# The last stage of a graph layer: part of v added on VectorE instead of GpSimd, and results added one step earlier

## The chip, the cores and the metric

The kernel runs on one core of a Trainium2 chip. The metric is the device time of one execution in microseconds. A core has five engines with instruction queues of their own: TensorE (PE, matmuls), VectorE (DVE), ScalarE (ACT), GpSimd (POOL) and SyncE (SP, which here only issues DMAs). Each queue runs in order, and queues meet at semaphores. TensorE's clock has two levels, 1.2 and 2.4 GHz; the profile shows the granted share of the upper one.

## The reference

One layer of a graph network over B = 16 graphs, N = 1024 nodes, D = 256 features, all in float32:

```
pre_u  = h @ W1[:d];  pre_v = h @ W1[d:]
hidden = relu(pre_u[:, :, None, :] + pre_v[:, None, :, :] + b1)       # b u v k
S      = sigmoid(hidden @ W2 + b2)                                    # b u v
a_t    = einsum('buv,bud->bvd', S * A, h)
m_t    = einsum('uv,bud->bvd', A, h) * h
out    = beta1 * h + beta2 * (a_t @ Wa + ba) + beta3 * (m_t @ Wm + bm)
```

A is 1024 x 1024 and mostly zero. h is the input x.

## The kernel before

Everything but the last sum over u is done ahead: `hWa_dram` holds beta2 * h @ Wa, `base_dram` all terms of the output that don't depend on S, and `sum_dram` (u, v, b) the part of the gate's argument that is not linear. The linear parts are kept apart: `of_u`, in on-chip memory for good, and `of_v`, a tile of 128 v by 16 b that is the same in all 128 partitions and is loaded anew for each group.

The last stage, the only one that the change touches, works on 64 tiles of 128 u by 128 v, each for 16 graphs. Eight tiles with the same v make a group (`vt`), `t` counts the u tiles in it, and `k = 8 * vt + t`. A tile passes four engines:

- SyncE loads `raw[k % 2]` (1 MB of `sum_dram`, L1440) and `adj_b[k % 5]` (64 KB of A, L1442). In group 0 it also loads `hWa_all` for that t (2 MB, L1444), which stays for all groups. At t == 0 it first waits until all adds of the group before are done and loads `of_v` (1 MB, L987). At t == 4 it waits until the results of the group before are stored, and loads `z` (2 MB of `base_dram`, L1447).
- GpSimd adds `of_v` to `raw` and writes the sum, turned from (v, b) to (b, v), into one of four buffers `masked[k % 4]` (L1457). It waits until TensorE is done with tile k - 4 (`step_done`).
- ScalarE applies the sigmoid, 16 instructions (L1513). After t == 3 it issues the store of `z` of the group before (L1505).
- VectorE multiplies by `adj_b` (L1475). After t == 1 it calls `finish(vt - 1)`: eight additions of 512 elements that add PSUM to `z` (L1466).
- TensorE: 16 products of 128 x 128 by 128 x 256, each as two matmul instructions, into eight PSUM banks that add up over the eight tiles of a group (L1493). At t == 0 each pair of products waits until `finish` has taken the old contents of its bank.

No order is written out but that of each queue's program. Semaphores: `raw_added` counts the adds, `gate_made` the sigmoids, `gate_masked` the masks, `gate_used` and `z_summed` TensorE's tiles, `z_ready` the z additions.

Of the kernel before, what the change touches and what calls it, by code (L numbers as in the profile page):

```python
# [5 lines left out]
def gnn_edges_kernel(nc, x, adj, W1, b1, W2, b2, Wa, ba, Wm, bm, beta1, beta2, beta3, out):  # L6
# [15 lines left out]
    ALU = mybir.AluOpType  # L22
# [43 lines left out]
    with ctx:  # L66
# [919 lines left out]
        def load_of_v(sp, vt):  # L986
            sp.dma_start(of_v[:].rearrange("p v b -> p (v b)"), linear_dram[1, vt * P:(vt + 1) * P, :]  # L987
                         .rearrange("(a v) b -> a (v b)", a=1).broadcast_to([P, P * B])).then_inc(of_v_loaded, 16)
# [408 lines left out]

        work.close()
        with ExitStack() as phase:
            RAW, GM, ADJ = 2, 4, 5  # L1400
            hWa_all = sb("hWa_all", [P, NT, B, D], scope=phase)
            raw = [sb(f"raw{i}", [P, P, B], scope=phase) for i in range(RAW)]
            adj_b = [sb(f"adj_b{i}", [P, P], scope=phase) for i in range(ADJ)]
            masked = [sb(f"masked{i}", [P, B, P], scope=phase) for i in range(GM)]
            z = sb("z", [P, B, D], scope=phase)
            z_psum = [pb(f"z_psum{i}", [P, BANK], scope=phase) for i in range(B // 2)]
            raw_loaded = [sem(f"raw_loaded{i}") for i in range(RAW)]
            adj_loaded = [sem(f"adj_loaded{i}") for i in range(ADJ)]
            hWa_loaded = [sem(f"hWa_loaded{i}") for i in range(NT)]
            u_ready = sem("u_ready")  # L1410
            raw_added = sem("raw_added")
            gate_made = sem("gate_made")
            z_loaded = sem("z_loaded")
            gate_masked = sem("gate_masked")
            gate_used = sem("gate_used")
            z_summed = sem("z_summed")
            z_ready = sem("z_ready")
            z_stored = sem("z_stored")
            sum_uv = sum_dram.rearrange("(u v) b -> u v b", v=N)

            def step_done(eng, k):
                vt, t = divmod(k, NT)
                if k < 0:
                    return
                if t == NT - 1:
                    eng.wait_ge(z_summed, (B // 2) * (vt + 1))
                else:
                    eng.wait_ge(gate_used, (NT - 1) * vt + t + 1)  # L1428

            with nc.Block() as block:  # L1430
                @block.sync
                def _(sp):
                    for vt in range(NT):
                        for t in range(NT):
                            k = vt * NT + t
                            if t == 0 and vt:
                                sp.wait_ge(raw_added, k)
                                load_of_v(sp, vt)
                            waits(sp, raw_added, k - RAW + 1)
                            sp.dma_start(raw[k % RAW][:], sum_uv[t * P:(t + 1) * P, vt * P:(vt + 1) * P, :]).then_inc(raw_loaded[k % RAW], 16)  # L1440
                            waits(sp, gate_masked, k - ADJ + 1)
                            sp.dma_start(adj_b[k % ADJ][:], adj[t * P:(t + 1) * P, vt * P:(vt + 1) * P]).then_inc(adj_loaded[k % ADJ], 16)  # L1442
                            if vt == 0:
                                sp.dma_start(hWa_all[:, t, :, :], hWa_dram[:, t * P:(t + 1) * P, :].rearrange("b p d -> p b d")).then_inc(hWa_loaded[t], 16)  # L1444
                            if t == 4:
                                waits(sp, z_stored, 16 * vt)
                                sp.dma_start(z[:], base_dram[:, vt * P:(vt + 1) * P, :].rearrange("b p d -> p b d")).then_inc(z_loaded, 16)  # L1447

                @block.gpsimd
                def _(pool):  # L1450
                    for vt in range(NT):
                        pool.wait_ge(of_v_loaded, 16 * (vt + 1))
                        for t in range(NT):
                            k = vt * NT + t
                            pool.wait_ge(raw_loaded[k % RAW], 16 * (k // RAW + 1))
                            step_done(pool, k - GM)
                            nc.gpsimd.tensor_tensor(masked[k % GM][:].rearrange("p b v -> p v b"), raw[k % RAW][:], of_v[:], ALU.add).then_inc(raw_added, 1)  # L1457

                @block.vector
                def _(dve):  # L1460
                    def finish(vt):
                        dve.wait_ge(z_loaded, 16 * (vt + 1))
                        for q in range(B // 2):
                            dve.wait_ge(z_summed, (B // 2) * vt + q + 1)
                            rows_ = z[:, 2 * q:2 * q + 2, :].rearrange("p b d -> p (b d)")
                            nc.vector.tensor_tensor(rows_, rows_, z_psum[q][:], ALU.add).then_inc(z_ready, 1)  # L1466

                    dve.wait_ge(of_u_loaded, 16)
                    nc.vector.tensor_scalar(of_u[:], of_u[:], half_sign[:, 0:1], betas[:, 3:4], ALU.mult, ALU.add).then_inc(u_ready, 1)
                    for vt in range(NT):  # L1470
                        for t in range(NT):
                            k = vt * NT + t
                            dve.wait_ge(adj_loaded[k % ADJ], 16 * (k // ADJ + 1))
                            dve.wait_ge(gate_made, k + 1)  # L1474
                            nc.vector.tensor_tensor(masked[k % GM][:], masked[k % GM][:],  # L1475
                                                    adj_b[k % ADJ][:].rearrange("p (a v) -> p a v", a=1).broadcast_to([P, B, P]),
                                                    ALU.mult).then_inc(gate_masked, 1)
                            if t == 1 and vt:
                                finish(vt - 1)
                    finish(NT - 1)  # L1480

                @block.tensor
                def _(pe):
                    for vt in range(NT):
                        for t in range(NT):
                            k = vt * NT + t
                            if vt == 0:
                                pe.wait_ge(hWa_loaded[t], 16)
                            pe.wait_ge(gate_masked, k + 1)
                            for b in range(B):  # L1490
                                if t == 0 and b % 2 == 0:
                                    waits(pe, z_ready, (vt - 1) * (B // 2) + b // 2 + 1)
                                last = nc.tensor.matmul(z_psum[b // 2][:, (b % 2) * D:(b % 2 + 1) * D], masked[k % GM][:, b, :],  # L1493
                                                        hWa_all[:, t, b, :], start=(t == 0 and b % 2 == 0), stop=(t == NT - 1),
                                                        skip_group_check=True)
                                if t == NT - 1 and b % 2:
                                    last.then_inc(z_summed, 1)
                            if t < NT - 1:
                                last.then_inc(gate_used, 1)

                @block.scalar
                def _(act):
                    def store(vt):
                        act.wait_ge(z_ready, (B // 2) * (vt + 1))
                        act.dma_start(out[:, vt * P:(vt + 1) * P, :].rearrange("b p d -> p b d"), z[:]).then_inc(z_stored, 16)  # L1505

                    act.wait_ge(u_ready, 1)
                    for vt in range(NT):
                        for t in range(NT):
                            k = vt * NT + t  # L1510
                            act.wait_ge(raw_added, k + 1)
                            for b in range(B):
                                last = nc.scalar.activation(masked[k % GM][:, b, :], masked[k % GM][:, b, :], ACT.Sigmoid,  # L1513
                                                            bias=of_u[:, t, b:b + 1], scale=half_sign[:, 0:1])
                            last.then_inc(gate_made, 1)
                            if t == 3 and vt:
                                store(vt - 1)
                    store(NT - 1)
                    act.wait_ge(z_stored, 16 * NT)
# [27 lines left out]
```

## Time and profile before

| what | value |
|---|---|
| time, median of 3 runs | 3941.08 us (3937.64 to 3946.14) |
| time of the profiled execution | 3951.05 us |
| its span | 3949.3 us |
| TensorE busy over the span | 3452.5 us (87%) |
| VectorE, ScalarE, GpSimd busy | 2832.8, 2318.1, 1859.7 us |
| last stage, from its first add to the end | 3368.0 to 3949.3 us |

The profile is one execution of the kernel. Busy times say how much of the span an engine ran; the idle time ahead of a group of instructions is shown with what ended it. PE is TensorE, DVE VectorE, POOL GpSimd, SPq and ACTq the DMAs that SyncE and ScalarE issue. L1475 is line 1475 of the kernel.

### The profile page before, as it was taken

To read this page: it belongs to the slowest core of one execution; us is meant where nothing else is said; L and a number is where in the kernel's file an instruction comes from. 1 tells how busy PE (TensorE), PEld (TensorE's weight loads), DVE (VectorE), ACT (ScalarE), POOL (GpSimd) and SP (SyncE) were. 2 spreads that over 40 slices of the span, in tenths; PEclk is the share of its full clock that TensorE was granted. 3 is DMA by queue.
4 is the path that set the end of the run, shared out by engine and by line. 5 is a ranking of instruction groups with operands and counts; after the bars stand their busy time and mean duration, and the time that the engine had idled before them with its cause. 6 is when DMAs were issued, how large, how long until landed. Compare 5 with 4: busy or idle time off the path is not lost. (4 is left out here: it accounts for less than half of the span.)

```text
span 3949.3 us, 56078 instructions
## 1 busy us (share of the span) xinstructions
PE 3452.5 (87%) x14232; PEld 2670.5 (68%) x14232; DVE 2832.8 (72%) x4788; ACT 2318.1 (59%) x14050; POOL 1859.7 (47%) x2338
## 2 busy tenths in 40 slices
PE   4977877887877949999999999999999999578898
PEld 2655555555555637887888888888888887567677
DVE  4455555555555358999999999999999999354534
ACT  0111111111111127998999999999999998577765
POOL 2222222212112125666666666666666665465664
PEclk9989988998988979999999999999999999789999
DMA  4545544555465577566765666765766653956564
GB/s 147 187 168 199 208 171 168 184 209 180 175 217 189 194 178 161 140 172 150 170 157 141 150 137 166 169 168 133 185 145 163 158 128 71 316 203 228 185 214 164
DMA packets 342892, 685.83 MB, mean 174 GB/s; under 512 B 38782, under 2 KB 252648, under 8 KB 319720
## 3 DMA queue, kind: packets, MB, share of 16 engines
q1 hardware_dynamic: 304544, 612.07, 53.6%
q0 software_dynamic: 21504, 53.31, 4.4%
q10 hardware_dynamic: 16512, 16.78, 1.3%
q8 instruction: 116, 1.90, 0.2%
q14 instruction: 216, 1.77, 0.2%
HBM read 444.01 MB, written 256.18 MB: 177 GB/s over the span
## 5 line engine op out<-in xcount | busy, mean ns | idle before, releaser
L1169 ACT ACTIVATE junk<-psum_a 128x128 f32<-128x128 f32 x6144 | 1605.3, 296 | 238.3 <-PE psum_a L1073 172.3
L1169 ACT ACTIVATION_READ_ACCUMULATOR junk<-psum_a 128x1 f32 x6144 | 1381.8, 227 | 0.0
L1114 DVE TENSOR_REDUCE group_sum<-psum_d 128x56 f32<-128x896 f32 x1024 | 1111.2, 1085 | 84.7 <-PE psum_d L1073 44.6
L1072 PE MATMUL psum_d<-u_t,pk 128*128 128x512 f32 x2560 | 1006.5, 393 | 62.2 <-DMA v_t<-rows_dram 33.0
L1073 PE MATMUL psum_d<-v_t,pk 128*128 128x512 f32 x2560 | 999.9, 391 | 0.0
L1218 POOL DMA_INDIRECT sum_dram<-total,idx_all x512 | 505.8, 988 | 228.0 <-POOL total L1229 124.1
L1072 PEld LDWEIGHTS psum_d<-u_t,pk 128*128 128x128 f32 x2560 | 482.2, 188 | 186.0 <-issue 50.2
L1072 PE MATMUL psum_a<-u_t,pk 128*128 128x512 f32 x1536 | 605.6, 394 | 0.0
L1073 PE MATMUL psum_a<-v_t,pk 128*128 128x512 f32 x1536 | 599.3, 390 | 0.0
L1493 PE MATMUL z_psum<-hWa_all,masked 128*128 128x256 f32 x2048 | 474.0, 396 | 118.1 <-DVE masked L1475 71.3
L849 POOL TENSOR_TENSOR own<-whole 128x256 f32<-128x256 f32 x128 | 92.4, 722 | 998.6 <-issue 729.4
L1073 PEld LDWEIGHTS psum_d<-v_t,pk 128*128 128x128 f32 x2560 | 482.6, 189 | 98.4
L1493 PEld LDWEIGHTS z_psum<-hWa_all,masked 128*128 128x128 f32 x2048 | 407.2, 200 | 184.9 <-DVE masked L1475 74.5
L603 PE MATMUL wide<-adj_sb,h 128*128 128x512 f32 x1024 | 511.6, 622 | 0.0
L1513 ACT ACTIVATE masked<-masked,of_u,half_sign 128x128 f32<-128x128 f32 x1024 | 399.0, 480 | 151.7 <-POOL masked L1457 151.7
L673 ACT COPY hWa<-ring 128x512 f32<-128x512 f32 x64 | 37.5, 586 | 715.4 <-PE ring L625 715.4
L1475 DVE TENSOR_TENSOR masked<-masked,adj_b 128x2048 f32<-128x2048 f32 x64 | 220.3, 3445 | 307.8 <-ACT masked L1513 307.8
L1457 POOL TENSOR_TENSOR masked<-raw,of_v 128x2048 f32<-128x2048 f32 x64 | 330.9, 5186 | 230.0 <-DMA raw<-sum_dram 169.2
L1211 POOL TENSOR_TENSOR fold<-group_sum,group_sign 128x256 f32<-128x256 f32 x256 | 189.7, 741 | 394.6 <-DVE group_sum L1141 392.8
L587 PE MATMUL ring<-W_k,hT 128*128 128x258 f32 x1024 | 277.6, 431 | 108.9 <-ACT whole L666 107.5
L1111 DVE TENSOR_REDUCE late_sum<-psum_d 128x4 f32<-128x512 f32 x512 | 347.0, 678 | 0.4 <-PE psum_d L1073 0.4
L1072 PEld LDWEIGHTS psum_a<-u_t,pk 128*128 128x128 f32 x1536 | 289.0, 188 | 77.6 <-ACT junk L1169 20.5
(207 smaller groups left out, 4039.7 us busy)
## 6 DMA issues: line engine op xcount, KB each, us to landing
u_t<-rows_dram SPq DMA_DIRECT2D x126, 1024.0 KB
rows_dram<-split SPq DMA_DIRECT2D x128, 512.0 KB, 3.3
sum_dram<-zero SPq DMA_DIRECT2D x128, 512.0 KB, 5.0
pk<-pick_dram SPq DMA_DIRECT2D x512, 128.0 KB, 2.7
raw<-sum_dram SPq DMA_DIRECT2D x64, 1024.0 KB, 7.0
v_t<-rows_dram SPq DMA_DIRECT2D x36, 1024.0 KB, 13.1
whole_dram<-whole SPq DMA_DIRECT2D x128, 256.0 KB, 3.8
pick_dram<-pick SPq DMA_DIRECT2D x128, 256.0 KB, 2.0
```

Source lines behind the costliest of these rows:

```text
L587: last = nc.tensor.matmul(ring[:, w * BANK:w * BANK + CW], hT[:, c, t * P:(t + 1) * P], W1_k[:, c, w, :], start=(c == 0), stop=(c == DT - 1))
L603: last = nc.tensor.matmul(wide[:, c * N + n * BANK:c * N + (n + 1) * BANK], h[b % 2][:, t, c * P:(c + 1) * P], adj_sb[:, t, n * BANK:(n + ...
L1072: nc.tensor.matmul(dst, pk[n % PKS][:, at:at + P], part(u_t[k % 2][:], b, LB), start=True, stop=False)
L1073: return nc.tensor.matmul(dst, pk[n % PKS][:, SLOTS + at:SLOTS + at + P], part(v_t[n % VG][:], b, LB), start=False, stop=True)
L1111: return nc.vector.tensor_reduce(out_, in_, AX, ALU.add, apply_absolute_value=True)
L1114: nc.vector.tensor_reduce(out_[:, :, 1:EG], in_[:, :, GW:LATE].rearrange("p b (g k) -> p b g k", k=GW), AX, ALU.add, apply_absolute_value= ...
L1169: last = nc.scalar.activation(junk[:, a % RING_A, k * LATE:(k + 1) * LATE], psum_a[a % RING_A][:, k * LATE:(k + 1) * LATE], ACT.Abs, accum ...
L1218: nc.gpsimd.indirect_dma_start(out=sum_dram[:, :], out_offset=bass.IndirectOffsetOnAxis(ap=at, axis=0), in_=sums, in_offset=None, bounds_c ...
L1457: nc.gpsimd.tensor_tensor(masked[k % GM][:].rearrange("p b v -> p v b"), raw[k % RAW][:], of_v[:], ALU.add).then_inc(raw_added, 1)
L1475: nc.vector.tensor_tensor(masked[k % GM][:], masked[k % GM][:], adj_b[k % ADJ][:].rearrange("p (a v) -> p a v", a=1).broadcast_to([P, B, P ...
L1493: last = nc.tensor.matmul(z_psum[b // 2][:, (b % 2) * D:(b % 2 + 1) * D], masked[k % GM][:, b, :], hWa_all[:, t, b, :], start=(t == 0 and ...
L1513: last = nc.scalar.activation(masked[k % GM][:, b, :], masked[k % GM][:, b, :], ACT.Sigmoid, bias=of_u[:, t, b:b + 1], scale=half_sign[:, ...
```

## The change

In the last stage the add of `of_v` goes from GpSimd's queue to VectorE's, where the add of tile k + 2 stands ahead of the mask of tile k (the adds of tiles 0 and 1 stand ahead of all). `finish(vt - 1)` stands ahead of the mask of t == 1 and of the add with it, where it stood behind the mask. SyncE loads adj_b ahead of raw. `MASKS` is 1, so that the new loops over parts of a mask run once, and the semaphore counts are as before.

```diff
-            RAW, GM, ADJ = 2, 4, 5
+            RAW, GM, ADJ, MASKS = 2, 4, 5, 1
...
+                            waits(sp, gate_masked, MASKS * (k - ADJ + 1))
+                            sp.dma_start(adj_b[k % ADJ][:], adj[t * P:(t + 1) * P, vt * P:(vt + 1) * P]).then_inc(adj_loaded[k % ADJ], 16)
                             waits(sp, raw_added, k - RAW + 1)
                             sp.dma_start(raw[k % RAW][:], sum_uv[t * P:(t + 1) * P, vt * P:(vt + 1) * P, :]).then_inc(raw_loaded[k % RAW], 16)
-                            waits(sp, gate_masked, k - ADJ + 1)
-                            sp.dma_start(adj_b[k % ADJ][:], adj[t * P:(t + 1) * P, vt * P:(vt + 1) * P]).then_inc(adj_loaded[k % ADJ], 16)
...
-                @block.gpsimd
-                def _(pool):
-                    for vt in range(NT):
-                        pool.wait_ge(of_v_loaded, 16 * (vt + 1))
-                        for t in range(NT):
-                            k = vt * NT + t
-                            pool.wait_ge(raw_loaded[k % RAW], 16 * (k // RAW + 1))
-                            step_done(pool, k - GM)
-                            nc.gpsimd.tensor_tensor(masked[k % GM][:].rearrange("p b v -> p v b"), raw[k % RAW][:], of_v[:], ALU.add).then_inc(raw_added, 1)
...
+                    def add_of_v(k):
+                        if k % NT == 0:
+                            dve.wait_ge(of_v_loaded, 16 * (k // NT + 1))
+                        dve.wait_ge(raw_loaded[k % RAW], 16 * (k // RAW + 1))
+                        step_done(dve, k - GM)
+                        nc.vector.tensor_tensor(masked[k % GM][:].rearrange("p b v -> p v b"), raw[k % RAW][:], of_v[:], ALU.add).then_inc(raw_added, 1)
+
+                    HB = B // MASKS
+                    for k in range(2):
+                        add_of_v(k)
                     for vt in range(NT):
                         for t in range(NT):
                             k = vt * NT + t
-                            dve.wait_ge(adj_loaded[k % ADJ], 16 * (k // ADJ + 1))
-                            dve.wait_ge(gate_made, k + 1)
-                            nc.vector.tensor_tensor(masked[k % GM][:], masked[k % GM][:],
-                                                    adj_b[k % ADJ][:].rearrange("p (a v) -> p a v", a=1).broadcast_to([P, B, P]),
-                                                    ALU.mult).then_inc(gate_masked, 1)
                             if t == 1 and vt:
                                 finish(vt - 1)
+                            if k + 2 < NT * NT:
+                                add_of_v(k + 2)
+                            dve.wait_ge(adj_loaded[k % ADJ], 16 * (k // ADJ + 1))
+                            for m in range(MASKS):
+                                rows_ = masked[k % GM][:, m * HB:(m + 1) * HB, :]
+                                dve.wait_ge(gate_made, MASKS * k + m + 1)
+                                nc.vector.tensor_tensor(rows_, rows_,
+                                                        adj_b[k % ADJ][:].rearrange("p (a v) -> p a v", a=1).broadcast_to([P, HB, P]),
+                                                        ALU.mult).then_inc(gate_masked, 1)
```

## Rows read from the trace of the kernel before

**Rows 1.** The page: its first line.

```profile
span 3949.3 us, 56078 instructions
```

**Rows 2.** Groups by line, last stage: busy us, mean ns; idle before, its releasers.

```profile
L1493 PE MATMUL z_psum<-hWa_all,masked 128*128 128x256 f32 x2048 | 474.0, 396 | 118.1 <-DVE masked L1475 71.3 <-DVE z L1466 46.8
...
L1513 ACT ACTIVATE masked<-masked,of_u,half_sign 128x128 f32<-128x128 f32 x1024 | 399.0, 480 | 151.7 <-POOL masked L1457 151.7
L1457 POOL TENSOR_TENSOR masked<-raw,of_v 128x2048 f32<-128x2048 f32 x64 | 330.9, 5186 | 230.0 <-DMA raw<-sum_dram 169.2 <-PE z_psum L1493 53.2 <-issue 7.5
L1475 DVE TENSOR_TENSOR masked<-masked,adj_b 128x2048 f32<-128x2048 f32 x64 | 220.3, 3445 | 307.8 <-ACT masked L1513 307.8
```

**Rows 3.** Windows by group, three of groups 1 to 6: length, busy times, clock, DMA.

```profile
3473.50:3538.70 65.20, 58.00 (x256) 50.06 (x257) 29.20 (x17) 46.11 (x120) 38.75 (x8) 0.97 0.59 209
...
3671.30:3744.70 73.40, 57.47 (x257) 49.67 (x257) 32.75 (x17) 53.43 (x138) 44.67 (x9) 0.90 0.57 201
...
3810.00:3877.50 67.50, 61.32 (x257) 52.46 (x257) 28.77 (x17) 49.97 (x129) 44.56 (x9) 0.90 0.59 210
```

**Rows 4.** Timeline of PE, last stage: start us, us, instructions, idle before.

```profile
3473.51 37.01 PE L1493 MATMUL z_psum<-hWa_all,masked 128*128 128x256 f32 x160 [14.83 <-DVE z L1466]
...
3604.80 36.23 PE L1493 MATMUL z_psum<-hWa_all,masked 128*128 128x256 f32 x160 [3.08 <-DVE z L1466]
...
3708.41 20.99 PE L1493 MATMUL z_psum<-hWa_all,masked 128*128 128x256 f32 x96 [0.66 <-DVE masked L1475]
...
3877.47 36.43 PE L1493 MATMUL z_psum<-hWa_all,masked 128*128 128x256 f32 x160 [2.23 <-DVE z L1466]
3917.94 22.67 PE L1493 MATMUL z_psum<-hWa_all,masked 128*128 128x256 f32 x96 [4.05 <-DVE masked L1475]
```

**Rows 5.** Windows behind a wait of PE; the clock is third from the end.

```profile
3645.00:3647.00 2.00, 1.86 (x5) 1.51 (x6) 1.62 (x2) 2.00 (x6) 0.00 (x0) 0.58 0.99 397
```

**Rows 6.** Timeline of DVE: group 3, and its last instruction.

```profile
3601.75 2.31 DVE L1475 TENSOR_TENSOR masked<-masked,adj_b 128x2048 f32<-128x2048 f32 x1 [4.26 <-ACT masked L1513]
3603.98 4.86 DVE L1466 TENSOR_TENSOR z<-z,z_psum 128x512 f32<-128x512 f32 x8
...
3614.88 5.37 DVE L1475 TENSOR_TENSOR masked<-masked,adj_b 128x2048 f32<-128x2048 f32 x1 [3.84 <-ACT masked L1513]
...
3940.65 0.69 DVE L1466 TENSOR_TENSOR z<-z,z_psum 128x512 f32<-128x512 f32 x1 [0.18 <-PE z_psum L1493]
```

**Rows 7.** Timeline of ACT, group 3: sigmoids of t3, store of z.

```profile
3608.51 2.04 ACT L1513 ACTIVATE masked<-masked,of_u,half_sign 128x128 f32<-128x128 f32 x5 [0.29 <-POOL masked L1457]
3610.19 0.38 ACTq L1505 DMA_DIRECT2D out_dram<-z  x1
```

**Rows 8.** Timeline of SP: of_v for group 1, then group 3.

```profile
3441.55 0.32 SPq L987 DMA_DIRECT2D of_v<-linear_dram  x1
...
3617.72 0.37 SPq L1447 DMA_DIRECT2D z<-base_dram  x1
...
3619.92 0.43 SPq L1442 DMA_DIRECT2D adj_b<-in_adj_dram  x1
...
3642.97 0.32 SPq L987 DMA_DIRECT2D of_v<-linear_dram  x1
```

**Rows 9.** Timeline of POOL: end of group 0, then groups 3 and 4.

```profile
3428.18 4.54 POOL L1457 TENSOR_TENSOR masked<-raw,of_v 128x2048 f32<-128x2048 f32 x1 [4.06 <-DMA raw<-sum_dram]
3436.98 4.55 POOL L1457 TENSOR_TENSOR masked<-raw,of_v 128x2048 f32<-128x2048 f32 x1 [4.26 <-DMA raw<-sum_dram]
3449.06 10.08 POOL L1457 TENSOR_TENSOR masked<-raw,of_v 128x2048 f32<-128x2048 f32 x2 [7.53 <-issue]
...
3628.36 9.06 POOL L1457 TENSOR_TENSOR masked<-raw,of_v 128x2048 f32<-128x2048 f32 x2 [10.25 <-DMA raw<-sum_dram]
...
3650.72 24.25 POOL L1457 TENSOR_TENSOR masked<-raw,of_v 128x2048 f32<-128x2048 f32 x4 [7.79 <-DMA raw<-sum_dram]
```

**Rows 10.** Source view of GpSimd's add: min/median/max ns, first and last start.

```profile
L1457 POOL TENSOR_TENSOR masked<-raw,of_v x64: 4528/4556/6631, 3368.0 to 3911.2; 128x2048 f32<-128x2048 f32 x64
```

More of the change, by code:

```diff
@@ L1488, in _ @@
                                 pe.wait_ge(hWa_loaded[t], 16)
-                            pe.wait_ge(gate_masked, k + 1)
                             for b in range(B):
+                                if b % (B // MASKS) == 0:
+                                    pe.wait_ge(gate_masked, MASKS * k + b * MASKS // B + 1)
                                 if t == 0 and b % 2 == 0:
@@ L1514, in _ @@
                                                             bias=of_u[:, t, b:b + 1], scale=half_sign[:, 0:1])
-                            last.then_inc(gate_made, 1)
+                                if (b + 1) % (B // MASKS) == 0:
+                                    last.then_inc(gate_made, 1)
                             if t == 3 and vt:
```

## The prediction

> **What bounds the kernel now.** I read the page first: the span is 3949.3 us, and the run's own time of 3951.05 us is 1.75 us more [rows 1]. The change touches only the last stage, so I cut that stage out with the view of groups by line. In it TensorE is busy 474.0 us over some 570, GpSimd's adds 330.9, VectorE's masks 220.3, ScalarE's sigmoids 399.0; TensorE is idle for two reasons: 71.3 us until a mask is done and 46.8 us until results of the group before are added [rows 2]. No other engine is close to full, so the stage is bound by TensorE plus the chains that make it wait.
>
> The windows by group show what those waits are worth. From one group's first matmul to the next one's it takes 65.2 to 67.5 us, once 73.4 [rows 3]. From the first start of group 1 to that of group 7, (3877.47 - 3473.51) / 6 = 67.3 us [rows 4]. TensorE alone would need far less: 96 matmuls (three tiles) ran in 20.99 us after a wait of 0.66 us, so a tile is at most 7.0 us; 160 ran in 36.23 us, of which part is a cold start. After a wait of 4.05 us the same 96 took 22.67 us [rows 4], and behind such a wait the granted clock is 0.58, half speed for most of it [rows 5]. So a long wait costs 22.67 - 20.99 = 1.68 us more, and a warm tile is (36.23 - 1.68) / 5 = 6.91 to 7.0 us; I take 6.95. Eight of them are 55.6 us: some 11.7 us of each group is waiting.
>
> Which wait ends last? I followed one group through four queues [rows 6 to 9]. The results of group 2 are added by 3608.84 (3603.98 + 4.86) [rows 6]; ScalarE issues their store at 3610.19 [rows 7]; SyncE, which stands behind that store, issues the load of z at 3617.72, 7.53 us later [rows 8]; the part for tile 5 is queued behind z, and its add starts at 3628.36, 10.64 us after z's issue [rows 9]. SyncE's next hold is of_v: issued at 3642.97, as soon as tile 7's add is done, and the next group's first add starts at 3650.72, 7.75 us later [rows 8, 9]. The loop through store, z, raw, add, of_v, raw, sigmoid, mask is as long as the group. It is a chain of transfers, not GpSimd's speed, though its 4.56 us lie on it several times.
>
> **The change, part by part.** I write S for the start of a group's tile 0 on TensorE, t0 to t7 for its tiles, and count from S.
>
> The add on VectorE. No row has its access pattern on this engine. The nearest in engine and size is the mask, two inputs in on-chip memory, 2048 elements, 2.31 us, and the next instruction starts 2.23 us after it (3603.98 - 3601.75) [rows 6]. The nearest in access pattern is the same add on GpSimd, 4528 ns at least [rows 10]. Bounds: 2.2 and 4.5 us. I take 2.23, since the mask shares engine, type and length, and on GpSimd this pattern is no dearer than its engine's size would suggest. VectorE then has 8 x (2.23 + 2.23) + 4.86 = 40.5 us of work in a group of 67: not the bound.
> The Trainium skill, SBUF — State Buffer, section "Door 1: The DMA port swizzle", says accesses that cross to a new 16-byte line pay a penalty; each element of this output does (512 bytes apart). VectorE: DVE Perf Modes, section "Mode 1× (REGULAR)", says the one-element-a-cycle mode takes odd strides as they come. By the first the add would approach GpSimd's bound and the kernel be slower, by the second it is the mask's; no row here decides it.
>
> GpSimd idle. Its adds and the masks get in each other's way: a mask that runs alone takes 2.31 us, one that falls into an add 5.37, and an add that falls into a mask up to 6.63 where one alone takes 4.56 [rows 6, 10]. That goes. What it is worth is inside the sums below, which use undisturbed durations.
>
> Results ahead of the mask of t1. Now VectorE can do the z additions only after the sigmoids and mask of t1; TensorE stands at S. After: after t6 of the group before ends (S - 6.95), VectorE adds t2, masks t0 and adds results: 0.1 + 2 x 2.23 + 4.86, ending at S + 2.45. Its first sums are ready at about S - 1.8, so TensorE goes from t7 to the next t0 without a stop. This wait (2.2 to 15 us a group [rows 4]) is gone, with its cold start.
>
> The price: order on VectorE. Before, the add of t5 could be late and hold only t5's sigmoids. Now the add of t5 stands ahead of the mask of t3, two tiles earlier, and blocks it. Step by step: results done S + 2.45; add of t3 to 4.7; ScalarE passes its 16 sigmoids and issues the store 1.68 later (3610.19 - 3608.51 [rows 7]), 6.4; z issued 7.53 later, 13.9; z and raw landed 10.64 later, plus one adj issue that now stands between them (0.43 [rows 8]), 25.0; add of t5 and mask of t3, 2 x 2.23 + 0.1, so t3 starts at 29.6. TensorE had finished t0 to t2 at 20.9: it waits 8.7 us and starts cold. t3 ends at 29.6 + 6.95 + 1.68 = 38.2. The add of t7 waits for it (four buffers): 40.6. of_v and the next raw, 7.75 plus 0.3 for the adj between them: 48.6. Add of next t0 and mask of t6: 53.2; t4 and t5 were done at 52.1, a wait of 1.1, too short to cool TensorE. t6 and t7: 67.1. So a group takes 67.1 us, against 67.3 on average, 66.1 without the disturbed one ((67.3 x 6 - 73.4) / 5).
>
> The adj load ahead of raw. Its wait (mask of tile k - 5) is always met before raw's (add of k - 2), as each add stands before the mask two tiles back. It costs only the 0.3 to 0.4 us used above.
>
> The first group is bound by loading hWa_all, 2 MB a tile, so its adds keep their pace: t6 at 3428.18, t7 at 3436.98, ended 3441.53 now, 3439.2 after [rows 9]. But each mask now stands behind the add two tiles on. Mask t4 ends 3432.6, mask t5 3441.4, t5 runs to 3448.5. of_v is issued 2.3 us earlier than at 3441.55 [rows 8]; its landing was 7.5 us later and shares the queue with the last hWa tile, so I take 3448 for the next raw, not 3449.06. Mask t6 3452.5, t6 (cold) to 3461.2, t7 to 3468.2. Group 1 would start at 3468.2, before 3473.5: 5.3 us gained.
>
> The last group has no of_v: t3 starts at S + 29.6, then five tiles and one cold start to 66.05, and the last z addition 0.86 on (0.17 + 0.69 [rows 6]): 66.9. Before: 3941.34 - 3877.47 = 63.9 [rows 4, 6]: 3.0 lost.
>
> Sum: -5.3 (first) - 6 x 0.2 (six groups, rounded: 67.3 - 67.1) + 3.0 (last) = -3.5 us. Against its own time: 3951.05 - 3.5 = 3947.5 for a profiled execution; the profiled one was 10 us above the median of 3941.1, so for the median I say 3937.6. I call 0.2% (7.9 us) what a measurement of this kernel can tell from no change; this is within it. One thing can shift it: were the 73.4 us group [rows 3] absent from ordinary runs, they have 7 us less to give, and the result is 3945, still no change.
>
> **The rivals.**
> *The store's chain is shorter than I sum.* If z and the raw behind it land 1.7 us sooner, or the wait before t3 does not cool TensorE, each group is 65.4 us: 7 x 1.7 = 12 us less, 3926. For: the chain has nine handovers rounded up. Against: 7.53 and 10.64 are measured in the same neighbourhood.
> *The chain is hidden altogether.* If t5's raw did not wait for the store, a group is 55.6 us, 7 x 11.5 = 80 us less, about 3857. Against: SyncE's order is unchanged and it does wait there today [rows 8].
> *The scattered output costs VectorE more* (slower). Adds of t2, t3, t5, t7 and the next t0 lie on the path: five a group, 33 in six groups and the last part. The price decides when it passes (3.5 + 7.9) / 33 = 0.35 us, that is an add over 2.6 us; at GpSimd's 4.5 us it is 33 x 2.3 = 76 us more, about 4013.
> The Trainium skill's rule of 16-byte lines (SBUF — State Buffer, the section above) is this rival's reason; no trace row of VectorE bears it out.
> *The wait before t3 spreads* (slower): the second hold, of_v, adds 2 us to each group, since both raw loads and of_v are issued together; with the six groups that load it 6 x 2 = 12 us, 3950.
> *The results-first order does nothing*, because TensorE was held by masks anyway. Then PE would still stop at S; at 3 us a group, 7 x 3 = 21 us, 3959.
>
> **How the numbers follow.** Forecast, either way about the disturbed group: 0.44. Shorter chain: 0.22; hidden: 0.08. Dearer output: 0.12. Spread or no use of the order: 0.14. Faster by over 0.2% is 0.30, within 0.44, slower 0.26. The range runs from the shorter chain less 3 us (3922) to the last rival (3959), and leaves out the hidden chain and the dearest output: 0.2 at most. It takes in adds up to 2.8 us.
>
> **What would show it.** Adds on VectorE at 2.2 to 2.3 us, masks all at 2.3. No stop of TensorE at a group's start; instead one of about 8.7 us before its fourth tile, at a granted clock near half behind it, released by the mask, and that mask behind an add that waited for raw. Groups of 67 us. The load of z some 14 us after the group's start. Group 1 about 5 us earlier. The prediction is wrong if the stop before t3 is under 5 or over 11 us, if the adds take over 2.6 us, or if of_v brings a second stop.

## The result, and the profile after

The changed kernel takes 4016.74 us (median of 4, 4009.55 to 4020.12), the kernel before 3939.36 us in the same comparison: a ratio of 1.0193, interval 1.0172 to 1.0213. It is 1.9% slower. I had forecast 3937.6 us and no change; the range to 3959 does not hold it.

The groups by line of the last stage of the changed kernel, answering to [rows 2]:

```profile
L1498 PE MATMUL z_psum<-hWa_all,masked 128*128 128x256 f32 x2048 | 488.0, 403 | 167.8 <-DVE masked L1481 167.8
...
L1518 ACT ACTIVATE masked<-masked,of_u,half_sign 128x128 f32<-128x128 f32 x1020 | 397.2, 480 | 214.8 <-DVE masked L1465 214.8
L1465 DVE TENSOR_TENSOR masked<-raw,of_v 128x2048 f32<-128x2048 f32 x63 | 233.5, 3707 | 214.8 <-DMA raw<-sum_dram 162.0 <-PE z_psum L1498 52.8
L1481 DVE TENSOR_TENSOR masked<-masked,adj_b 128x2048 f32<-128x2048 f32 x64 | 145.8, 2279 | 2.1 <-ACT masked L1518 2.1
```

Three readings. The mask is down from a mean of 3445 ns to 2279: with GpSimd idle nothing gets in its way. TensorE no longer waits for z, but for masks it waits 167.8 us where the two waits of before were 118.1 (both sums hold the wait for the stage's first mask, 44.2 and 36.2 us). And VectorE's add takes 3707 ns, not the 2.3 us of the mask. Its source view says that every one of the 64 does (min/median/max ns):

```profile
L1465 DVE TENSOR_TENSOR masked<-raw,of_v x64: 3631/3710/3775, 3363.1 to 3971.6; 128x2048 f32<-128x2048 f32 x64
```

The timeline of PE, from t3 of group 1, from t1 of group 2 and at the end (group 7), answering to [rows 4]:

```profile
3498.38 23.32 PE L1498 MATMUL z_psum<-hWa_all,masked 128*128 128x256 f32 x96 [10.07 <-DVE masked L1481]
...
3551.19 15.62 PE L1498 MATMUL z_psum<-hWa_all,masked 128*128 128x256 f32 x64 [2.68 <-DVE masked L1481]
3575.31 22.41 PE L1498 MATMUL z_psum<-hWa_all,masked 128*128 128x256 f32 x96 [8.51 <-DVE masked L1481]
3601.71 22.74 PE L1498 MATMUL z_psum<-hWa_all,masked 128*128 128x256 f32 x96 [3.99 <-DVE masked L1481]
3627.12 14.08 PE L1498 MATMUL z_psum<-hWa_all,masked 128*128 128x256 f32 x64 [2.67 <-DVE masked L1481]
...
3937.41 14.08 PE L1498 MATMUL z_psum<-hWa_all,masked 128*128 128x256 f32 x64 [2.70 <-DVE masked L1481]
3961.43 37.70 PE L1498 MATMUL z_psum<-hWa_all,masked 128*128 128x256 f32 x160 [9.94 <-DVE masked L1481]
```

Each group has three stops: before t3 (8.4 to 10.1 us), before t6 (3.6 to 4.5 us), and before t1 of the next (2.7 us). The first is the one that I forecast, at 8.7 us, and TensorE comes out of it cold, as the window behind it shows (third from the end, the granted clock; compare [rows 5]):

```profile
3575.31:3577.31 2.00, 2.00 (x5) 1.64 (x6) 2.00 (x1) 2.00 (x6) 0.00 (x0) 0.50 0.85 352
```

The second I had put at 1.1 us and warm; at 4 us TensorE starts cold behind it: 96 matmuls take 22.74 us where they took 20.99 [rows 4]. The third I had not seen; behind it the 64 matmuls of t1 and t2 took 14.08 us in four groups and 15.5 to 15.6 in three. From group 1's t3 to group 7's a group is (3961.43 - 3498.38) / 6 = 77.2 us long, against 67.3 before [rows 4] and 67.1 in my sum.

How the stops come about shows in the queue of VectorE; here in group 2, from the additions of group 1's results on, and under it that of SyncE:

```profile
3540.53 4.87 DVE L1456 TENSOR_TENSOR z<-z,z_psum 128x512 f32<-128x512 f32 x8
3545.31 3.71 DVE L1465 TENSOR_TENSOR masked<-raw,of_v 128x2048 f32<-128x2048 f32 x1
3548.84 2.29 DVE L1481 TENSOR_TENSOR masked<-masked,adj_b 128x2048 f32<-128x2048 f32 x1
3551.03 3.74 DVE L1465 TENSOR_TENSOR masked<-raw,of_v 128x2048 f32<-128x2048 f32 x1
3554.58 2.31 DVE L1481 TENSOR_TENSOR masked<-masked,adj_b 128x2048 f32<-128x2048 f32 x1
3569.51 3.63 DVE L1465 TENSOR_TENSOR masked<-raw,of_v 128x2048 f32<-128x2048 f32 x1 [12.62 <-DMA raw<-sum_dram]
3572.99 2.27 DVE L1481 TENSOR_TENSOR masked<-masked,adj_b 128x2048 f32<-128x2048 f32 x1
```
```profile
3558.24 0.37 SPq L1447 DMA_DIRECT2D z<-base_dram  x1
3558.66 2.02 SPq L1440 DMA_DIRECT2D adj_b<-in_adj_dram  x1
3560.72 0.43 SPq L1442 DMA_DIRECT2D raw<-sum_dram  x1
```

The add of t5 (3569.51) waits 12.62 us for raw, which stands in SyncE's queue behind z and z behind the store; the mask of t3 (3572.99), whose sigmoids have long been there, stands behind that add. TensorE starts at 3575.31. This is step for step the chain of the prediction. What differs most is the add: the next instruction starts some 3.5 us after it (3548.84 - 3545.31 = 3.53, 3554.58 - 3551.03 = 3.55), not 2.23.

### The profile page after: what moved, and what is told of

It is laid out like the page before. It is cut to its first block and busy times, and to the rows that moved or that the text cites. A ratio compares the mean times of both kernels' runs of the same rounds, so it can differ in the third digit from the quotient of the medians.

```text
span 4007.8 us, 56078 instructions
## 1 busy us (share of the span) xinstructions
PE 3465.6 (86%) x14232; PEld 2675.4 (67%) x14232; DVE 2984.1 (74%) x4852; ACT 2323.4 (58%) x14050; POOL 1532.7 (38%) x2274
## 5 line engine op out<-in xcount | busy, mean ns | idle before, releaser
L1498 PE MATMUL z_psum<-hWa_all,masked 128*128 128x256 f32 x2048 | 488.0, 403 | 167.8 <-DVE masked L1481 167.8
L1465 DVE TENSOR_TENSOR masked<-raw,of_v 128x2048 f32<-128x2048 f32 x64 | 237.1, 3705 | 216.8 <-DMA raw<-sum_dram 164.0
L1073 PEld LDWEIGHTS psum_a<-v_t,pk 128*128 128x128 f32 x1536 | 289.1, 188 | 57.0
```

The costliest lines, as they stand in the source:

```text
L1073: return nc.tensor.matmul(dst, pk[n % PKS][:, SLOTS + at:SLOTS + at + P], part(v_t[n % VG][:], b, LB), start=False, stop=True)
L1465: nc.vector.tensor_tensor(masked[k % GM][:].rearrange("p b v -> p v b"), raw[k % RAW][:], of_v[:], ALU.add).then_inc(raw_added, 1)
```

## The experiments

Ratios are to the kernel before, run beside each; the interval is 95%. The kernel before gave 3939 to 3946 us in the four comparisons, so differences between runs of different comparisons are taken from the ratios, at 3940 us for 1.

**Is it the scattered output, and what does the queue cost without it?** The add writes densely:

```diff
-                        nc.vector.tensor_tensor(masked[k % GM][:].rearrange("p b v -> p v b"), raw[k % RAW][:], of_v[:], ALU.add).then_inc(raw_added, 1)
+                        nc.vector.tensor_tensor(masked[k % GM][:].rearrange("p b v -> p (b v)"), raw[k % RAW][:].rearrange("p v b -> p (v b)"), of_v[:].rearrange("p v b -> p (v b)"), ALU.add).then_inc(raw_added, 1)
```

> The changed kernel with VectorE's add writing its result densely, in the order (v, b) in which it reads; the turn to (b, v) is left out, so the gates belong to the wrong places, and everything else is as changed. Theory 1 (the 3.71 us of the add are the scattered output): the add takes 2.29 us like the mask, each group 1.4 us less on each of five adds and one cold start less, 67 to 68 us instead of 76 to 78, the kernel 3936 to 3948 us. Theory 2 (the add costs 3.71 us for its two large inputs, whatever it writes): adds stay at 3.7 us and the time at 4016. Theory 3 (the loss is the order of VectorE's queue, whatever the add costs): adds at 2.3 us but the kernel still above 3980.

Measured: 3955.78 us, ratio 1.0026 (1.0016 to 1.0036). The add's source view and TensorE's timeline, groups 1, 2 and 7:

```profile
L1465 DVE TENSOR_TENSOR masked<-raw,of_v x64: 2280/2292/2293, 3363.9 to 3912.3; 128x2048 f32<-128x2048 f32 x64
```
```profile
3494.23 22.75 PE L1498 MATMUL z_psum<-hWa_all,masked 128*128 128x256 f32 x96 [8.67 <-DVE masked L1481]
3518.35 35.09 PE L1498 MATMUL z_psum<-hWa_all,masked 128*128 128x256 f32 x160 [1.37 <-DVE masked L1481]
3562.14 22.92 PE L1498 MATMUL z_psum<-hWa_all,masked 128*128 128x256 f32 x96 [8.69 <-DVE masked L1481]
3586.78 35.09 PE L1498 MATMUL z_psum<-hWa_all,masked 128*128 128x256 f32 x160 [1.72 <-DVE masked L1481]
...
3902.71 37.11 PE L1498 MATMUL z_psum<-hWa_all,masked 128*128 128x256 f32 x160 [8.51 <-DVE masked L1481]
```

The turn alone costs 1.0193 - 1.0026 = 1.7%, some 66 us: nearly all of the loss. With it out, the kernel does what the prediction drew: a stop of 8.5 to 9 us before t3, one of 1 to 1.7 us before t6 behind which 160 matmuls run warm (35.09 us), and none at t1; groups of (3902.71 - 3494.23) / 6 = 68.1 us. Theory 2 and 3 fall. The median lies 8 us above the top of my 3936 to 3948 us.

**Can the turn be moved to the reads?**

```diff
-                        nc.vector.tensor_tensor(masked[k % GM][:].rearrange("p b v -> p v b"), raw[k % RAW][:], of_v[:], ALU.add).then_inc(raw_added, 1)
+                        nc.vector.tensor_tensor(masked[k % GM][:], raw[k % RAW][:].rearrange("p v b -> p b v"), of_v[:].rearrange("p v b -> p b v"), ALU.add).then_inc(raw_added, 1)
```

> The changed kernel with the turn moved from the output to the inputs of VectorE's add: it reads raw and of_v in steps of 64 bytes and writes densely; the whole of the reference is computed. If only scattered writes are dear, the add takes 2.3 us and the kernel 3936 to 3948 us. If steps cost the same on either side, the add stays at 3.7 us and the time at 4016; if each of two inputs pays, it is above 3.7 us, and each 0.5 us more is worth some 33 x 0.5 = 17 us.

Measured: 4020.03 us, ratio 1.0184 (1.0161 to 1.0207), the same as the changed kernel; its source view:

```profile
L1465 DVE TENSOR_TENSOR masked<-raw,of_v x64: 3589/3734/3817, 3370.2 to 3986.7; 128x2048 f32<-128x2048 f32 x64
```

Reads in steps of 64 bytes cost what writes in steps of 512 do, and two inputs in steps no more than one output: the turn has its price on either side.

**Where does the price begin?** Eight forms of the add in one kernel. The forms share the tiles, so its total time (3983.25 us, one run) tells nothing of any one of them.

```diff
-                        nc.vector.tensor_tensor(masked[k % GM][:].rearrange("p b v -> p v b"), raw[k % RAW][:], of_v[:], ALU.add).then_inc(raw_added, 1)
+                        m_, r_, o_ = masked[k % GM][:].rearrange("p b v -> p (b v)"), raw[k % RAW][:].rearrange("p v b -> p (v b)"), of_v[:].rearrange("p v b -> p (v b)")
+                        TT = nc.vector.tensor_tensor
+                        def stepped(x, s):
+                            return x.rearrange("p (x s) -> p s x", s=s)
+                        def rows(x, n):
+                            return x.rearrange("p (s x) -> p s x", s=n)
+                        n = k % 8
+                        if n == 0:
+                            ins = TT(m_, r_, o_, ALU.add)
+                        elif n == 1:
+                            ins = TT(stepped(m_, 2), rows(r_, 2), rows(o_, 2), ALU.add)
+                        elif n == 2:
+                            ins = TT(stepped(m_, 4), rows(r_, 4), rows(o_, 4), ALU.add)
+                        elif n == 3:
+                            ins = TT(stepped(m_, 16), rows(r_, 16), rows(o_, 16), ALU.add)
+                        elif n == 4:
+                            ins = TT(stepped(m_, 128), rows(r_, 128), rows(o_, 128), ALU.add)
+                        elif n == 5:
+                            ins = TT(rows(m_, 16), stepped(r_, 16), rows(o_, 16), ALU.add)
+                        elif n == 6:
+                            ins = TT(rows(m_, 4), stepped(r_, 4), stepped(o_, 4), ALU.add)
+                        else:
+                            ins = TT(rows(m_, 128), rows(r_, 128), rows(o_, 128), ALU.add)
+                        ins.then_inc(raw_added, 1)
```

> A measurement: the changed kernel with eight forms of VectorE's add, tile k taking form k mod 8, all over the same 2048 elements; outputs land permuted, so only the adds' durations are read. Forms: 0 all dense; 1, 2, 3, 4 write in steps of 8, 16, 64, 512 bytes (as 2, 4, 16, 128 rows) and read densely; 5 reads raw in steps of 64 bytes; 6 reads both inputs in steps of 16 bytes; 7 all dense, but described as 128 rows of 16. Theory 1 (an element that lies in another 16-byte line than the one before costs more): 0, 1 and 7 take 2.3 us, 2 to 6 all 3.7. Theory 2 (the short rows of the description cost, whatever the step): 0 to 3 take 2.3 us, 4 and 7 3.7. Theory 3 (only a large step costs): 1 and 2 take 2.3 us, 3 something between, 4 3.7.

The source views of the eight lines, in the order of the forms 0 to 7:

```profile
L1473 DVE TENSOR_TENSOR masked<-raw,of_v x8: 2291/2292/2293, 3370.2 to 3883.9; 128x2048 f32<-128x2048 f32 x8
L1475 DVE TENSOR_TENSOR masked<-raw,of_v x8: 2285/2286/2293, 3379.8 to 3888.3; 128x2048 f32<-128x2048 f32 x8
L1477 DVE TENSOR_TENSOR masked<-raw,of_v x8: 3802/3926/3954, 3388.6 to 3895.7; 128x2048 f32<-128x2048 f32 x8
L1479 DVE TENSOR_TENSOR masked<-raw,of_v x8: 3639/3652/3698, 3397.3 to 3906.5; 128x2048 f32<-128x2048 f32 x8
L1481 DVE TENSOR_TENSOR masked<-raw,of_v x8: 3696/3711/3807, 3406.9 to 3912.2; 128x2048 f32<-128x2048 f32 x8
L1483 DVE TENSOR_TENSOR masked<-raw,of_v x8: 3607/3614/3620, 3421.6 to 3930.4; 128x2048 f32<-128x2048 f32 x8
L1485 DVE TENSOR_TENSOR masked<-raw,of_v x8: 3844/3851/3911, 3430.5 to 3936.2; 128x2048 f32<-128x2048 f32 x8
L1487 DVE TENSOR_TENSOR masked<-raw,of_v x8: 2292/2292/2293, 3439.2 to 3945.3; 128x2048 f32<-128x2048 f32 x8
```

Steps of 8 bytes are free (2286 ns), steps of 16 bytes cost the most (3926), 64 and 512 bytes somewhat less (3652, 3711). One input in steps of 64 bytes takes 3614, both in steps of 16 bytes 3851. Short rows are not the cause: 128 rows of 16, dense, take 2292 (form 7), and four rows of 512 in steps of 16 bytes pay in full (form 2). Theory 1 holds in all eight forms; steps of 12 bytes were not tried, and steps of 8 bytes still put two elements into each 16 bytes. This is the rule of 16-byte lines that the prediction weighed, from the Trainium skill's SBUF — State Buffer, section "Door 1: The DMA port swizzle"; the trace agrees with the rule, and the price, which the page does not give for VectorE, is 1.32 to 1.63 us for 2048 elements. The other rule that I set against it (the Trainium skill's VectorE: DVE Perf Modes, section "Mode 1× (REGULAR)") holds only for what works, not for what it costs.

**The results ahead of the mask, taken back.**

```diff
-                            if t == 1 and vt:
-                                finish(vt - 1)
                             if k + 2 < NT * NT:
                                 add_of_v(k + 2)
...
                                                         ALU.mult).then_inc(gate_masked, 1)
+                            if t == 1 and vt:
+                                finish(vt - 1)
```

> The changed kernel with the results of the group before added behind the mask of t1 again, as before the change. Theory 1 (that part of the change gives something, as it takes TensorE's stop at a group's start away): the results come 3.54 + 2.28 us later, and TensorE's next group starts later; less what the earlier add of t3 gives back, 2 to 3 us a group, 4030 to 4037 us. Rival (the store behind t3's sigmoids sets the group, and that hardly moves): 4016, within 0.2%.

Measured: 4017.85 us, ratio 1.0180 (1.0157 to 1.0202): my expectation was wrong, the rival right. The groups by line show an exchange:

```profile
L1498 PE MATMUL z_psum<-hWa_all,masked 128*128 128x256 f32 x2048 | 498.2, 409 | 165.0 <-DVE masked L1479 118.6 <-DVE z L1456 46.4
```

TensorE stops for z at each group's start again, and for masks so much less (118.6 us, not 167.8). Results ahead of the mask is worth nothing to the changed kernel by itself.

**The hold on SyncE.**

```diff
-                            if t == 4:
+                            if t == 6:
                                 waits(sp, z_stored, 16 * vt)
```

> The changed kernel with SyncE's wait for the store, and the load of z behind it, moved from t == 4 to t == 6. Theory 1 (the loads of raw for t5 on stand behind the store of the results, and VectorE's mask of t3 behind the add of t5): the 8.5 to 10 us stop before each fourth tile goes, the stop lands two tiles later and is smaller; about 10 us a group less, 3940 to 3955 us. Rival (raw is late by its own 7 us and its two buffers, store or not): stop before t3 stays at 8 us and the time at 4016.

Measured: 3933.99 us, ratio 0.9973 (0.9963 to 0.9983). Against the changed kernel's 1.0193 this is 2.2%, 87 us, and 6 us under my range. The kernel is now a little faster than before the change, with the add still at 3.73 us (its median). TensorE's timeline over one group, from t1:

```profile
3616.44 27.89 PE L1498 MATMUL z_psum<-hWa_all,masked 128*128 128x256 f32 x128 [2.70 <-DVE masked L1481]
3644.67 7.17 PE L1498 MATMUL z_psum<-hWa_all,masked 128*128 128x256 f32 x32 [0.33 <-DVE masked L1481]
3656.08 22.57 PE L1498 MATMUL z_psum<-hWa_all,masked 128*128 128x256 f32 x96 [4.24 <-DVE masked L1481]
3681.35 27.89 PE L1498 MATMUL z_psum<-hWa_all,masked 128*128 128x256 f32 x128 [2.70 <-DVE masked L1481]
```

The stop before t3 is gone; those before t6 (4.24, the load of of_v) and t1 (2.70) stay. The group is 64.9 us here (3681.35 - 3616.44), and 66.3 on average of the six. The edit moves the wait for the store and the 2 MB load of z together, so it does not divide the gain between them. In group 2 of the changed kernel, above, raw's buffer for t5 comes free with the add of t3 at 3549.02; z is issued 9.2 us after that, and the add of t5 starts 11.3 us after z's issue.

**The order of adj_b and raw, taken back.**

```diff
-                            waits(sp, gate_masked, MASKS * (k - ADJ + 1))
-                            sp.dma_start(adj_b[k % ADJ][:], adj[t * P:(t + 1) * P, vt * P:(vt + 1) * P]).then_inc(adj_loaded[k % ADJ], 16)
                             waits(sp, raw_added, k - RAW + 1)
                             sp.dma_start(raw[k % RAW][:], sum_uv[t * P:(t + 1) * P, vt * P:(vt + 1) * P, :]).then_inc(raw_loaded[k % RAW], 16)
+                            waits(sp, gate_masked, MASKS * (k - ADJ + 1))
+                            sp.dma_start(adj_b[k % ADJ][:], adj[t * P:(t + 1) * P, vt * P:(vt + 1) * P]).then_inc(adj_loaded[k % ADJ], 16)
```

> The changed kernel with the load of adj_b behind that of raw again, as before the change. My sum had 0.3 to 0.4 us for the adj load ahead of raw at two places in a group: 7 x 0.7 = 5 us less, 4011 us. Rival (SyncE's issues behind z are held up until z is under way, so one more issue costs nothing): 4016 us; rival 2 (the order matters more, since adj's small rows hold raw up): 15 us or more less, 4001 us.

Measured: 4003.74 us, ratio 1.0148 (1.0127 to 1.0168), 0.45% or 18 us under the changed kernel's, whose interval begins at 1.0172: more than my 5 us, and rival 2 is nearest. SyncE's and VectorE's timelines in one group, and TensorE's t3 in groups 1 and 7:

```profile
3639.47 0.37 SPq L1447 DMA_DIRECT2D z<-base_dram  x1
3639.89 1.84 SPq L1440 DMA_DIRECT2D raw<-sum_dram  x1
3641.77 0.43 SPq L1442 DMA_DIRECT2D adj_b<-in_adj_dram  x1
```
```profile
3650.15 3.64 DVE L1465 TENSOR_TENSOR masked<-raw,of_v 128x2048 f32<-128x2048 f32 x1 [12.05 <-DMA raw<-sum_dram]
```
```profile
3504.26 23.54 PE L1498 MATMUL z_psum<-hWa_all,masked 128*128 128x256 f32 x96 [9.82 <-DVE masked L1481]
...
3954.82 37.34 PE L1498 MATMUL z_psum<-hWa_all,masked 128*128 128x256 f32 x160 [9.74 <-DVE masked L1481]
```

The issue right behind z takes 1.2 to 2.2 us, whichever it is. In the changed kernel that is adj_b's, so raw is issued 2.48 us after z; here 0.42 us. Yet the add comes little sooner. From z's issue to the add it is 10.68 us here and 11.27 in the group shown above, but this is the shortest here: on average of the seven groups it is 11.0 against 11.2. More lies behind of_v, where every issue takes 0.3 to 0.8 us in either order: from of_v's issue to the next add it is 7.2 us on average of six, against 8.1. Together that is 1.1 of the 2.1 us by which a group is shorter ((3954.82 - 3504.26) / 6 = 75.1). The other 1.0 is TensorE's own time: the 96 matmuls behind the stop before t3, and those behind the stop before t6, take 22.7 and 22.6 us on average of the six groups, against 23.2 and 23.2. Why the landing behind of_v is longer with adj_b ahead is open.

**The two order questions on the kernel before, adds on GpSimd.** First results ahead of the mask of t1 alone:

```diff
                         for t in range(NT):
                             k = vt * NT + t
+                            if t == 1 and vt:
+                                finish(vt - 1)
                             dve.wait_ge(adj_loaded[k % ADJ], 16 * (k // ADJ + 1))
...
-                            if t == 1 and vt:
-                                finish(vt - 1)
```

> The kernel before, adds on GpSimd, with one part of the change alone: results of the group before are added ahead of the mask of t1. Theory 1 (the store of the results stands behind t3's sigmoids on ScalarE, and these keep their time, so the loop through store, z and raw stays): TensorE's stop at a group's start goes, another wait takes most of it; 0 to 2 us a group, 3930 to 3944 us. Rival (the loop starts where the results are added): 6.3 + 2.3 us a group less, 3885 us.

Measured: 3940.20 us, ratio 0.9988 (0.9979 to 0.9998). Then z at t == 6 alone (the diff as above):

> The kernel before with SyncE's wait for the store and its load of z moved from t == 4 to t == 6, nothing else. Theory 1 (store, z and raw behind it set the group's length in the kernel before too): raw of t5 and t6 come some 15 us sooner, groups 4 to 5 us shorter, 3905 to 3915 us. Rival (that hold is hidden behind TensorE there, only the changed kernel has it on its path): 3941 us, within 0.2%.

Measured: 3939.98 us, ratio 0.9991 (0.9981 to 1.0001): my expectation was wrong. And both:

> The kernel before, adds on GpSimd, with results ahead of the mask of t1 and z loaded at t == 6. If the two waits are one after another in the loop, each edit gives what it gives alone or more: 8 to 9 us a group less, 3875 to 3890 us, faster than all others. If results early gives nothing beside z later, 3905 to 3915 us.

Measured: 3887.50 us, ratio 0.9851 (0.9832 to 0.9870): the fastest, 59 us under the kernel before, where the two edits alone gave 5 and 4, the second within its interval of nothing. TensorE's timeline, two rows of each, in the order in which they stand here (results early, z later, both):

```profile
3645.61 58.02 PE L1493 MATMUL z_psum<-hWa_all,masked 128*128 128x256 f32 x256 [7.17 <-DVE masked L1477]
...
3777.47 58.66 PE L1493 MATMUL z_psum<-hWa_all,masked 128*128 128x256 f32 x256 [8.42 <-DVE masked L1477]
```
```profile
3605.50 57.08 PE L1493 MATMUL z_psum<-hWa_all,masked 128*128 128x256 f32 x256 [9.10 <-DVE z L1466]
3671.80 58.06 PE L1493 MATMUL z_psum<-hWa_all,masked 128*128 128x256 f32 x256 [9.21 <-DVE z L1466]
```
```profile
3592.69 55.49 PE L1493 MATMUL z_psum<-hWa_all,masked 128*128 128x256 f32 x256 [2.67 <-DVE z L1466]
3650.91 57.18 PE L1493 MATMUL z_psum<-hWa_all,masked 128*128 128x256 f32 x256 [2.73 <-DVE z L1466]
```

Each kernel with one edit has one long stop in most groups, of 7 to 9 us, by a mask that comes late (raw behind z) or by z additions that come late (behind the mask of t1). I read this as two loops of nearly the same length: cutting one leaves the other to set the group, at 65.8 and 66.7 us on average. Cutting both leaves 2.7 us, and groups of 58.2 us (3650.91 - 3592.69), TensorE's own 55.5 and the stop; 59.0 on average, since behind some of these stops TensorE is slower (57.18 us).

**VectorE again, with the orders mended.** The dense add with z at t == 6 (two diffs from above, the turn left out):

> The changed kernel with both: VectorE's add written densely (the turn left out, so not the reference's result), and z loaded at t == 6. If the price of the scattered output and the order of SyncE's queue are all that the changed kernel loses, its groups come near TensorE's own 55.6 us: 57 to 59 us, the kernel 3875 to 3890 us, level with the version on GpSimd with both orders mended. If VectorE's queue itself, with the add ahead of the mask, costs more, it stays above 3905 us.

Measured: 3892.13 us, ratio 0.9868 (0.9852 to 0.9885), level with the version on GpSimd (0.9832 to 0.9870) and 2 us above my range. So what VectorE's queue costs beyond the turn and the place of z's load is too small to tell here. And the changed kernel, its scattered add kept, with z at t == 6 and adj_b behind raw:

> The changed kernel, adds on VectorE as they are, with z loaded at t == 6 and adj_b loaded behind raw: the changed kernel with both orders on SyncE mended. The two gave 82 and 13 us less alone. If they add up, 3921 us. If z at t == 6 has taken away the place where the order of adj and raw counts, 3928 to 3934. It would have to come to 3888 us or less for VectorE to be as good a place for the add as GpSimd; I expect it not to, by 35 us, since its adds and masks need 8 x 5.8 + 4.9 = 51 us of a group and stand in one queue.

Measured: 3928.66 us, ratio 0.9957 (0.9941 to 0.9974), not told apart from z at t == 6 alone (0.9973), and above the 0.9928 that the two gains would add up to (87 and 18 us by the ratios; the 82 and 13 of the expectation are differences of medians of different comparisons): beside z at t == 6 the order of adj_b and raw is worth little. It is 1.1% behind the version on GpSimd, 42 us.

## Why the prediction was wrong

**The bottleneck and the chain: right.** TensorE plus a loop of transfers; the stop moved from the group's start to t3, I said 8.7 us, it is 8.4 to 10.1, and 8.5 to 9.1 with the dense add. That raw behind the store and z is its cause is shown by z at t == 6, where the stop is gone. The times of the chain were taken from one group: 10.64 us from z's issue to the add is the shortest of the seven of before (mean 10.95), 7.75 us behind of_v the longest of six (mean 7.50). That the two errors cancel is luck. One reading was too wide: of the 71.3 us that TensorE waits for masks, 36.2 are the wait for the stage's first one, ahead of all groups.

**"I take 2.23" for the add on VectorE: the step that failed.** It is 3.54 us, shown by the dense add, which takes 2.29 us and gives 66 of the 77 us back. I chose the nearest row by engine and size over the nearest by access pattern, although a rule spoke for a price. The rival of the dearer output was the right one; its threshold, an add over 2.6 us, was passed. Two of the signs that the prediction named against itself came true: adds over 2.6 us, and a second stop with of_v. The pattern on GpSimd, 4.56 us, could not show it.

**The price in sum.** A group grew by 77.2 - 67.3 = 9.9 us. Of that five adds on the path are 5 x 1.31 = 6.6. With two of these adds ahead of it the second stop grew from the 1.1 us of my sum to 4, and TensorE starts cold behind it: 22.74 us for 96 matmuls against 20.99 [rows 4], 1.7 more. That cold start was at nothing in my sum. The rest, 1.6 and the 0.2 that I had as a gain, is mostly TensorE too. From the start of t3 to the add of t7, which waits for t3's end, it is 9.5 us on average of the six groups where I had 8.7; from the start of t6 to the add of t2 it is 9.4, where a tile, a cold start and 0.1 are 8.8. In some groups the clock stays low for longer behind the stop: 2 to 4 us behind the start of t3 the granted clock is 0.77 in group 2 (from 3577.31) and 0.50 in group 3 (from 3653.24), and the 96 matmuls take 22.41 and 23.68 us:

```profile
3577.31:3579.31 2.00, 2.00 (x9) 1.69 (x8) 2.00 (x2) 2.00 (x6) 0.00 (x0) 0.77 0.00 0
```
```profile
3651.24 23.68 PE L1498 MATMUL z_psum<-hWa_all,masked 128*128 128x256 f32 x96 [10.04 <-DVE masked L1481]
```

The landings have 0.2 of it: 11.2 and 8.1 us on average, 19.3 together, against my 19.1. The dense kernel, too, is 1.0 us a group above my sum (68.1 against 67.1). That the rival's 4013 us came close is luck: it had an add of 4.5 us and no cold start, and with the price that was measured, 33 x 1.31 = 43 us, its sum gives 3981.

**A stop that I did not see.** By my own numbers the mask of t1 was done at S + 2.45 + 2 x 2.25 + 0.1 = 7.0, and t0 ends at S + 6.95: a slack of nothing. With adds of t2 and t3 each 1.3 us longer, t1 stops for 2.7 us. I count it as no loss of its own here, since the stop before t3 follows in any case and ends with the mask of t3, but with that stop gone (z at t == 6) it remains.

**GpSimd idle: right in kind.** All masks run at 2.26 to 2.31 us; what that gave in time no run shows by itself.

**adj_b ahead of raw: under-sized.** 0.3 to 0.4 us at two places, 5 us in all; measured 18, and the two intervals together allow 6 to 29. The landing behind z is 0.2 us longer with adj_b ahead, that behind of_v 0.9; the rest stands in TensorE's time.

**The first and last group.** The first gained 4.0 us, not 5.3: from the first add to the start of group 1 it took 3473.5 - 3368.0 = 105.5 us before and 3464.6 - 3363.1 = 101.5 after. (3464.6 is t1's start of 3474.23 less its wait of 2.70 and a tile of 6.95.) The last lost 8.2, not 3.0: from t0 of group 7 to the end of the last z addition it took 63.9 us before and 3999.9 - (3937.41 - 2.70 - 6.95) = 72.1 after. With six groups of 9.9 the stage is 63 us longer; the profiled span grew by 58.5, because the stage began 4.9 us earlier.

**Profile and median.** The medians are 77 us apart, the profiled executions 58.5: that of before was 10 us above its median, that of after 7 below. So part of the difference lies between executions, as the prediction had allowed in saying that the 73.4 us group may be absent. The dense kernel shows the same: its profile gives 0.8 us less than before's, its ratio 10 us more. Which groups differ in executions without a profile is open.

## What to carry to other kernels

When an instruction moves to another engine, take its price from a row with the same access pattern on that engine, or bound it; size and type are not enough: on VectorE an element step of 16 bytes or more cost 58 to 71% more. A dearer instruction can also lengthen a stop so far that the next engine starts cold; price that too. In an in-order queue look at what stands ahead of the wait, twice: an add set ahead of a mask inherits the add's transfer, and a load behind a store's wait holds all loads behind it. Two loops of equal length hide each other, so that an edit that gives nothing alone may be half of the best one: here 5 and 4 us alone, 59 together. And a landing read from one group can be its shortest: average over the groups before you call a cause.

## What the runs showed of the hardware

- VectorE's add of two float32 operands of 2048 elements takes 2.29 us for dense patterns and for steps of 8 bytes, and 3.61 to 3.93 us as soon as one operand steps by 16 bytes or more, whether it is read or written, one or two of them (16 bytes 3.85 to 3.93, 64 and 512 bytes 3.61 to 3.73).
- The DMA issue of SyncE right behind that of the 2 MB load of z took 1.2 to 2.2 us, before and after the change, where most others take 0.3 to 0.4. Giving that place to the 64 KB load of adj_b instead of the 1 MB load of raw made raw's landing only 0.2 us later.
- TensorE's clock after a stop of 8 to 10 us came back after a different time from group to group: 2 to 4 us behind the start it was 0.77 in one and 0.50 in the next. Behind stops of 2.7 us it was slower in some groups (64 matmuls in 15.5 to 15.6 us) and not in others (14.08).
- ScalarE's DMA issue does not wait for the sigmoids ahead of it in its queue: in all seven groups of the changed kernel the store went out 1.67 or 1.68 us after the first of 16 had started, and 16 take 6.3 us.
